# A macaron layer on one core: tile 7 of x enters its experts one position sooner, and its load moves behind the store of tile 2

## The chip, the cores and the metric

The kernel runs on one core of a Trainium2 chip. The metric is the device time of one execution in microseconds (us). The kernel before takes 1252.88 us, the median of three runs that lie between 1252.73 and 1253.44 us.

## The reference

Input x is 4 x 1024 rows of 128 numbers, all in float32. Three sublayers follow one another, each added to the row it reads:

```
x = x + 0.5 * ffn(layernorm(x))      # mixture of 8 experts
x = x + mamba(layernorm(x))          # selective scan along the 1024 rows of a sequence
x = x + 0.5 * ffn(layernorm(x))      # the same experts again

ffn(x):   cw = softmax(x @ w_router) * softmax(x @ w_gating / 0.1);  cw = cw / (sum(cw) + 1e-9)
          out = sum over e of  cw[e] * ((silu(x @ w_gate[e]) * (x @ w_up[e])) @ w_down[e])
          # w_gate, w_up: 8 x 128 x 512;  w_down: 8 x 512 x 128
mamba(x): xs, z = split(x @ W_in)                      # 256 + 256 channels
          xc = silu(conv of 4 taps along the rows(xs) + conv_b)
          dt = softplus((xc @ W_x)[:, :64] @ W_dt + b_dt);  B, C = the other 2 x 16 columns of xc @ W_x
          h[n] = exp(dt * A[n]) * h[n] + dt * xc * B[n]    # 16 states n, one row after the other
          y = sum over n of h[n] * C[n] + xc * D;   out = (y * silu(z)) @ W_out
```

Each of the two ffn sublayers uses all 8 experts for every row, so most of the arithmetic is theirs.

## The kernel before, in words

The 4096 rows are cut into 8 tiles of 512 rows (two for each sequence). An expert pass over one tile is called a position. There are 16: kind 0 is the first ffn of a tile, kind 1 the second, and the table `ORDER` (line 36) says which comes when. A tile's mamba part lies between its two passes and runs beside the positions of other tiles. It needs the tile's kind 0 output (`x1`), and its output (`x2`) is what kind 1 reads. The scan carries a state from an even tile to the odd one behind it.

A position has 32 slots, one for each of 8 experts and 4 chunks of 128 hidden columns. Chunk number i counts through all positions, so position 9 (counted from 0) has the chunks 288 to 319. In a slot TensorE (PE) does three things: the gate product of chunk i + 2 (`first_g`, lines 839 to 842, three matmuls PS<-XH,WG), the up product of chunk i (`first`, the same lines, PS<-XH,WU) and the down product of chunk i - 2 (`down`, line 920, PS<-WD,HB). Between them ScalarE (ACT) applies silu to the gate product (line 1306) and VectorE (DVE) multiplies it with the up product (line 1113, "the multiply of chunk i" from here on). The up product of chunk i + 2 goes to the PSUM bank of that of chunk i, so it waits for the multiply of chunk i. The result of each expert is weighed on ACT (line 1331) or on DVE (line 1106) and added to the tile by a transfer that accumulates (line 1439, issued by GpSimd, POOL).

The order of all instructions is not written by hand. The function `timetable()` walks through the slots with a rough clock for each engine and appends steps to one list. Every engine's program is that list, filtered, so each engine works strictly in the list's order and waits on semaphores. The steps that matter here, with their lines:

- `ln_sum`, `ln_square`, `ln_x` (1262, 1270, 1276): layernorm on ACT. `ln_sum` is the first reader of a tile, and waits for its load or for `x1` or `x2`.
- `ln_t` (861) transposes the rows on PE. `p_xh` (1284) and `p_xl` (1171) write the two halves XH from which the next position's products read.
- `b_soft` (1380, 1382): the softplus of the mamba part, with its own activation table. `b_add` (1444) and `b_dx` (1183) follow it.
- For each of the 16 states: `s_b` (1200, DVE) reads the rows of B from the ring BCB of three buffers, `s_scan` (1211, two on DVE) reads the decays DA, which `s_da` makes on ACT (1401, two states at a time), and `s_hc` (1219, DVE) multiplies with C from the same BCB buffer. The load of BCB (`bc_load`, 799) for state m is issued by SyncE (SP) once `s_hc` of state m - 3 is done. States are numbered through all tiles: tile 4 has 64 to 79.
- `out` (823) stores a finished tile, and `x_load` (816) brings in one of the tiles 5 to 7. Both are issued by SP, as are all `bc_load`s. The ring XT has five buffers, so tile 7 is loaded to the buffer of tile 2, and line 815 makes SP wait until the store of tile 2 has landed.

Of the kernel before, what the change touches and what calls it, by code (L numbers as in the profile page):

```python
# [25 lines left out]
XR = 5  # L26
# [6 lines left out]
EPS_LN = 1e-5  # L33
EPS_CW = 1e-9

ORDER = [(0, 0), (0, 1), (0, 2), (0, 3), (1, 0), (0, 4), (1, 1), (0, 5), (1, 2), (0, 6), (1, 3), (0, 7), (1, 4), (1, 5), (1, 6), (1, 7)]
NPOS = len(ORDER)
ENDS = (0, NPOS - 1)
POSITION = {kt: p for p, kt in enumerate(ORDER)}

PREP = 8
LATER = 20
LOADR = 0
LATE = 26
LEAD = 2.0
LAST = 2
# [20 lines left out]
def timetable():  # L67
# [6 lines left out]
    clock = {"pe": 0.0, "v": 0.0, "a": 0.0, "p": 0.0}  # L74
    free = [(0.0, b, None) for b in range(NB)]

    def step(*what, after=0.0, **work):

        steps.append(what)
        for e, c in work.items():  # L80
            clock[e] = max(clock[e], after) + c
            after = clock[e] + SIGNAL[e]
        return after
# [5 lines left out]
    def until(at):  # L89
        while clock["pe"] < at:  # L90
            yield False
# [5 lines left out]
    def take():  # L97
        while not free or free[0][0] > clock["pe"]:
            yield False
        return free.pop(0)[1:]  # L100
# [7 lines left out]
    def rows_of_x():  # L108

        while xn["lock"] or clock["pe"] < xn["at"]:  # L110
            yield False
        xn["lock"] = True

    def norm(b, what):
        while ln["lock"]:
            yield False
        ln["lock"] = True
        q = norms[0]
        norms[0] += 1
        yield from rows_of_x()  # L120
        yield from calm()
        if q == 0:
            at = step("ln_first", b, what, after=4.0, v=1.5, p=1.2)
            yield "first"
            at = step("ln_first_x", b, after=at, v=.7, a=.9)
        else:
            at = step("ln_sum", q, b, xn["by"], what, after=clock["pe"], a=1.6)
            yield True
            yield from calm()
            at = step("ln_square", q, b, after=at, a=1.6, p=2.0)  # L130
            yield from until(at + .3)
            at = step("ln_x", q, b, after=at, a=1.5)
        ln["lock"] = False
        yield from until(at + 0.7)
        bk = yield from take()
        at = step("ln_t", q, bk, pe=.6)
        xn.update(by=("m_tr", q + 1), lock=False)
        return q, bk[0], at

    def prep(p):  # L140
        kind, t = ORDER[p]
        q, b, at = yield from norm(t % XR, ("x", t) if kind == 0 else ("x2", t))
        at = step("p_xh", p, q, b, after=at, a=.52)
        yield from until_v(at + LATEST)
        at = step("p_xl", p, b, after=at, v=.61)
        give(b, "v_xl", p + 1, at)
        inputs.add(p)
        yield "inputs"
        yield from until(at)
        bk = yield from take()  # L150
        at = step("p_logits", p, bk, pe=.55, a=1.2)
        give(bk[0], "a_lr", p + 1, at)
        yield "logits"
        yield from until_v(at)
        at = step("p_max", p, bk[0], after=at, v=1.0)
        yield True
        if p == 0:
            yield from until(at + FIRST)
        yield from calm()
        at = step("p_exp", p, after=at, a=3.0)  # L160
        yield from until_v(at)
        at = step("p_norm", p, after=at, v=.4)
        yield True
        step("p_sum", p, v=.3)
        yield True
        at = step("p_cw", p, v=.35)
        if p in TURNS:
            streams["rows"] = weights_rows(p, at)
# [38 lines left out]
    def tail(p):  # L207
        kind, t = ORDER[p]
        if p * E + E - 1 in TURNED:
            weigh(p * E + E - 1)  # L210
        while "turn" in streams:
            yield False
        at = turned_at[p] if p * E + E - 1 in TURNED else weigh(p * E + E - 1)
        if kind == 0:
            x1[t] = at
        else:
            yield from until(at)
            step("out", t)

    def before(t):  # L220

        haste.add("before")
        q, b, at = yield from norm(t % XR, ("x1", t))
        haste.clear()
        at = step("b_xn", t, q, b, after=at, a=.52)
# [73 lines left out]
    def calm():  # L299
        while clock["a"] > clock["pe"] + CALM:  # L300
            yield False
# [59 lines left out]

    streams = {}
    rows_at, turned_at, weighed_at = {}, {}, {}
    asked = [0]

    def row_loads():
# [35 lines left out]
    def side(but=None):  # L402
        mamba_streams()
        for k in ("rows", "turn", "tail", "prep", "closing"):
            while k != but and advance(k) is True:
                pass
        decays()
        turn[0] += 1
        if "scans" in streams and (haste or turn[0] % (3 if passed[0] < NS // 2 else 1) == 0):
            advance("before")  # L410
        fill(clock["pe"] + LEAD + 1.0)

    def fill(at):

        while clock["v"] + 1.0 < at:
            mamba_streams()
            if advance("scans") is not True and advance("before") is not True:
                break
# [25 lines left out]
    def high(i):  # L444
        on = {"a": .53} if i // SLOTS in SCALAR_PARTS else {"v": .35}
        hi_at[i] = step("h_hi", i, after=h_at[i], **on)
    for i in range(total):
        p, r = divmod(i, SLOTS)
        if i + AHEAD < total:
            at = step("first_g", i + AHEAD, after=sil_at.get(i + AHEAD - NG, 0.0), pe=.69)  # L450
            sil_at[i + AHEAD] = step("silu", i + AHEAD, after=at, a=.52)
            side()
        fill(sil_at[i])
        at = step("first", i, after=h_at.get(i - 2, 0.0), pe=.69)
        clock["v"] = max(clock["v"], at, sil_at[i]) + .61
        h_at[i] = clock["v"] + SIGNAL["v"]
        if i in TURNED_SLOTS and p in SCALAR_PARTS:
            high(i)
        if i - 1 in hi_at:
            step("h_lo", i - 1, after=hi_at[i - 1], v=.6)  # L460
        if i in TURNED_SLOTS and p not in SCALAR_PARTS:
            high(i)
        side()
        if i >= LAG:
            step("down", i - LAG, after=h_at[i - LAG], pe=.7 if i - LAG in TURNED_SLOTS else .9)
            nd += 1
            if nd % FC == BEGIN_LATER and nd // FC - 1 in TURN_BEGINS:
                weigh(nd // FC - 1)
            if (nd + 1) % PAIR == 0 and nd + 1 in TURNED_SLOTS:
                on = {"a": .31} if (nd + 1) // SLOTS in SCALAR_PARTS else {"v": .2}  # L470
                step("wd_hi", nd + 1, **on)
                if "v" in on:
                    step("wd_lo", nd + 1, v=.4)
            if nd % PAIR == 0 and nd in TURNED_SLOTS and nd // SLOTS in SCALAR_PARTS:
                step("wd_lo", nd, v=.33)
            row_loads()
            if nd % SLOTS == 0:
                streams["tail"] = tail(nd // SLOTS - 1)
            elif nd % FC == 0:
                if nd % SLOTS == FC:  # L480
                    finish("prep")
                if nd // FC - 1 not in TURN_BEGINS:
                    weigh(nd // FC - 1)
        if p == 0:
            e = (r + 1) // 4 + 1
            if r % 4 == 3 and 3 <= e < E:
                step("w_split", e, (0,), a=.6, v=.7)
            e = r // 4 + 1
            if e < E and r % 4 == (0 if e < 3 else 1):
                step("w_split", e, (0, 1) if e < 3 else (1,), a=.6, v=.7)  # L490
                if e + 3 < E:
                    step("w_load", e + 3)
            if r == 6:
                step("small_load")
            if r % 2 and 25 <= r <= 29:
                step("set", (r - 25) // 2, v=1.4)
        if r == LOADR and p + 1 < NPOS and ORDER[p + 1][0] == 0 and ORDER[p + 1][1] >= XR:
            step("x_load", ORDER[p + 1][1])
        if p + 1 < NPOS and r >= (PREP if p != 1 else LATER) and p + 1 not in prepared:
            kind, t = ORDER[p + 1]  # L500
            if kind == 1 and r == LATE:
                while t not in x2:
                    side()
                    clock["pe"] += .3
            if kind == 0 or t in x2:
                prepared.add(p + 1)
                streams["prep"] = prep(p + 1)
        if r == SLOTS - 3:
            finish("prep", lambda: p + 1 in inputs)
        side()  # L510
# [973 lines left out]
```

## Time and profile before

| | us |
|---|---|
| median of three runs | 1252.88 |
| the profiled execution | 1252.7 |
| its span, first to last instruction | 1250.9 |
| PE busy / DVE busy / ACT busy / POOL busy | 1244.1 / 1131.1 / 1017.1 / 388.4 |
| PE waits that end between 130 and 1181 us of the span | 0.6 |

Times of rows are us from the start of the span. What the profiled execution's time has beyond its span, 1.8 us, lies outside the program's instructions. PE's matmuls overlap in the pipeline, and their ends are modelled, so the start of a row says more than its length: as long as PE is not held up, a slot begins every 2.28 us (the first up matmuls of two chunks stand at 751.30 and 753.58 us). The PE clock that was granted is 1.0 throughout.

### The profile page before, as it was taken

What the parts mean: (1) busy time and instruction counts of PE and PEld (TensorE: products, weight loads), DVE (VectorE), ACT (ScalarE), POOL (GpSimd) and SP (SyncE); (2) the same over time, 40 slices, a digit from 0 to 9 for tenths busy, and PEclk for the clock granted to TensorE, in tenths of its full rate; (3) what the DMA queues carried; (4) which work ended last, traced back from release to release, by engine and by line L of the source; (5) the groups of instructions that cost most, each with busy time, mean ns of one, the idle gap of its engine ahead of it and who ended that gap; (6) DMA issues with size and microseconds to landing.
All of it is one profiled execution on the core that took longest, in us unless ns stands there. A gap on an engine that the chain in (4) does not pass through costs nothing.

```text
span 1250.9 us, 20830 instructions
## 1 busy us (share of the span) xinstructions
PE 1244.1 (99%) x7311; PEld 1076.0 (86%) x7311; DVE 1131.1 (90%) x1524; ACT 1017.1 (81%) x2079; POOL 388.4 (31%) x455
## 2 busy tenths in 40 slices
PE   9999999999999999999999999999999999999998
PEld 6887888888888888888888888888888888888887
DVE  5857699999999999999999999999999989998476
ACT  6777988888987887989978899798987979765664
POOL 0010134234333333334234333352434433332100
PEclk9999999999999999999999999999999999999999
DMA  7412368797878787878898798987979887895132
GB/s 225 105 24 42 87 132 172 144 196 161 168 143 178 161 174 151 177 153 172 164 201 160 153 194 172 186 172 151 199 148 190 154 160 158 161 191 112 28 75 51
DMA packets 116809, 185.90 MB, mean 149 GB/s; under 512 B 11264, under 2 KB 31840, under 8 KB 116704
## 3 DMA queue, kind: packets, MB, share of 16 engines
q0 software_dynamic: 55760, 101.74, 46.1%
q1 hardware_dynamic: 60944, 82.83, 26.4%
q8 instruction: 57, 0.93, 0.3%
q14 instruction: 48, 0.39, 0.1%
HBM read 80.15 MB, written 2.67 MB: 66 GB/s over the span
## 4 chain that ended last, share of the span: by engine, by line
PE 96%; ACT 2%; DVE 1%; issue 1%; DMA 0%; POOL 0%; DVEq 0%; ACTq 0%
PE PS L920 32%; PE PS L839 19%; PE PS L842 19%; PE PS L840 19%; PE PS L969 1%; PE PS L954 1%; PE PS L912 1%; PE PS L914 1%; PE PS L910 1%; PE PS L861 1%; PE PS L871 1%; ACT DA L1401 0%; PE PS L961 0%; ACT HB L1306 0%; DVE HL L1069 0%
## 5 line engine op out<-in xcount | busy, mean ns | idle before, releaser
L920 PEld LDWEIGHTS PS<-WD,HB 128*128 128x128 f32 x3616 | 472.2, 191 | 37.6 <-issue 0.5
L920 PE MATMUL PS<-WD,HB 128*128 128x128 f32 x3616 | 476.0, 274 | 0.0
L1113 DVE TENSOR_TENSOR HB<-PS,HB 128x512 f32<-128x512 f32 x512 | 348.3, 681 | 85.7 <-PE PS L842 72.8
L1306 ACT ACTIVATE HB<-PS 128x512 f32<-128x512 f32 x512 | 294.6, 597 | 111.2 <-PE PS L842 108.7
L1456 POOL DMA_DIRECT2D Y<-HS x252 | 222.1, 958 | 369.2 <-DVE HS L1219 186.4
L839 PE MATMUL PS<-XH,WG 128*128 128x512 f32 x512 | 238.7, 466 | 0.8 <-DVE WG L1120 0.6
L1439 POOL DMA_DIRECT2D XT<-YE x111 | 105.4, 949 | 318.9 <-ACT YE L1331 166.8
L839 PE MATMUL PS<-XH,WU 128*128 128x512 f32 x512 | 203.7, 398 | 0.0
L842 PE MATMUL PS<-XH,WG 128*128 128x512 f32 x512 | 202.2, 395 | 0.0
L842 PE MATMUL PS<-XH,WU 128*128 128x512 f32 x512 | 201.6, 394 | 0.0
L840 PE MATMUL PS<-XH,WG 128*128 128x512 f32 x512 | 200.3, 391 | 0.0
L840 PE MATMUL PS<-XH,WU 128*128 128x512 f32 x512 | 200.3, 391 | 0.0
L1401 ACT ACTIVATE DA<-XS,aneg 128x512 f32<-128x512 f32 x256 | 164.3, 713 | 0.8
L1211 DVE TENSOR_TENSOR_SCAN HS<-DA,car,HS 128x512 f32<-128x512 f32 x128 | 161.8, 1275 | 0.0
L1219 DVE TENSOR_TENSOR HS<-BCB,HS 128x1024 f32<-128x1024 f32 x128 | 156.1, 1220 | 1.4
L1200 DVE TENSOR_TENSOR HS<-BCB,DX 128x1026 f32<-128x1026 f32 (+1 forms) x128 | 155.5, 1220 | 0.2
L1211 DVE TENSOR_TENSOR_SCAN HS<-DA,HS 128x513 f32<-128x513 f32 x128 | 153.8, 1217 | 0.1
L840 PEld LDWEIGHTS PS<-XH,WU 128*128 128x128 f32 x512 | 96.5, 188 | 22.6 <-issue 0.5
L842 PEld LDWEIGHTS PS<-XH,WU 128*128 128x128 f32 x512 | 96.0, 187 | 22.8
L839 PEld LDWEIGHTS PS<-XH,WU 128*128 128x128 f32 x512 | 96.1, 188 | 22.7 <-issue 0.5
L842 PEld LDWEIGHTS PS<-XH,WG 128*128 128x128 f32 x512 | 96.1, 188 | 22.6 <-DVE XH L1171 0.4
L1306 ACT ACT_TABLE_LOAD x87 | 111.6, 1283 | 2.1 <-PE PS L842 0.6
(133 smaller groups left out, 1343.7 us busy)
## 6 DMA issues: line engine op xcount, KB each, us to landing
BCB<-BCD SPq DMA_DIRECT2D x128, 512.0 KB, 5.3
Y<-HS POOLq DMA_DIRECT2D x252, 256.0 KB, 6.3
XT<-YE POOLq DMA_DIRECT2D x111, 256.0 KB, 4.9
YE<-CWD SPq DMA_DIRECT2D x15, 256.0 KB, 4.7
XS<-DX POOLq DMA_DIRECT2D x7, 512.0 KB, 9.0
AT<-YE POOLq DMA_DIRECT2D x11, 256.0 KB, 3.3
XT<-in_L_attn_x_dram SPq DMA_DIRECT2D x8, 256.0 KB, 6.6
WD<-in_L_ffn_w_down_dram SPq DMA_DIRECT2D x8, 256.0 KB, 6.4
```

The costliest lines, as they stand in the source:

```text
L839: pe.matmul(o, w[0], m[0], start=True, stop=False)
L840: pe.matmul(o, w[1], m[0], start=False, stop=False)
L842: pe.matmul(o, w[0], m[1], start=False, stop=True).then_inc(S[sem], 1)
L920: z = pe.matmul(part(g, j), HB[:, i % NH, j * P:(j + 1) * P], WD[:, e, c, :], start=c == 0 and j in firsts, stop=c == FC - 1 and j in lasts)
L1113: v.tensor_tensor(H, up(i), H, ALU.mult).then_inc(S["v_h"], 1)
L1200: v.tensor_tensor(HS[:, m % HR, :, 0:w], rows.unsqueeze(1).broadcast_to([P, 2, w]), DX[:, t % 2, :, 0:w], ALU.mult).then_inc(S["v_db"], 1)
L1211: v.tensor_tensor_scan(H, DA[:, m % NA, j, 0:w], H, car[:, j, n:n + 1] if t % 2 else 0.0, ALU.mult, ALU.add).then_inc(S["v_sc"], 1)
L1219: v.tensor_tensor(H, BCB[:, m % BR, 1, :].unsqueeze(1).broadcast_to([P, 2, T]), H, ALU.mult).then_inc(S["v_hc"], 1)
L1306: a.activation(HB[:, i % NH, :], gate(i), ACT.Silu).then_inc(S["a_sil"], 1)
L1401: z = a.activation(DA[:, m % NA, j, 0:T], XS[:, t % 2, j, 3:3 + T], ACT.Exp, scale=aneg[:, j, n:n + 1])
L1439: gp.dma_start(to, buffer(g), accum_op=ALU.add).then_inc(S["c_acc"], 16)
L1456: gp.dma_start(Y[:, t % 2, j, :], HS[:, m % HR, j, 0:T], accum_op=ALU.add).then_inc(S[f"c_y{j}"], 16)
```

## The change

Positions 10 and 11 change places. Before, position 10 is the second pass of tile 3 and position 11 the first pass of tile 7. Now tile 7 comes first. Its load was issued at slot 0 of the position before its pass. Now it is issued at slot 2 or later, as soon as the store of the tile five before has been issued in the list, and the clock by which `ln_sum` of the loaded tile is placed takes 7 us for that store and 8 us for the load.

```diff
-ORDER = [... (0, 6), (1, 3), (0, 7), (1, 4), (1, 5), (1, 6), (1, 7)]
+ORDER = [... (0, 6), (0, 7), (1, 3), (1, 4), (1, 5), (1, 6), (1, 7)]
...
-LOADR = 0
+LOADR = 2
+STORED = 7.0
+LOADED = 8.0
...
     def norm(b, what):
...
+        if what[0] == "x":
+            yield from until(loaded_x.get(what[1], 0.0))
         yield from rows_of_x()
         yield from calm()
...
             step("out", t)
+            stored_out[t] = clock["pe"]
...
-        if r == LOADR and p + 1 < NPOS and ORDER[p + 1][0] == 0 and ORDER[p + 1][1] >= XR:
-            step("x_load", ORDER[p + 1][1])
+        if r >= LOADR and p + 1 < NPOS and ORDER[p + 1][0] == 0:
+            t = ORDER[p + 1][1]
+            if t >= XR and t not in asked_x and t - XR in stored_out:
+                asked_x.add(t)
+                loaded_x[t] = max(clock["pe"], stored_out[t - XR] + STORED) + LOADED
+                step("x_load", t)
```

The lines of the engines' code move down by ten, so L799 becomes L809, and L1306 becomes L1316. Before position 9 only the loads of tiles 5 and 6 move, each by one or two places among the `bc_load`s. From slot 7 of position 9 on, the list differs at many places.

The first place is SP's queue around the store of tile 2, at the start of position 9. Before:

```order
L799 DMA BCB<-BCD 128x2x512 [waits v_hc] x2
L823 DMA out_dram<-XT 128x4x128 [waits c_acc]
L799 DMA BCB<-BCD 128x2x512 [waits v_hc] x4
L799 DMA BCB<-BCD 128x2x512 [waits v_hc,c_bcd]
L799 DMA BCB<-BCD 128x2x512 [waits v_hc] x3
L816 DMA XT<-in_L_attn_x_dram 128x4x128 [waits o_x]
```

Now:

```order
L809 DMA BCB<-BCD 128x2x512 [waits v_hc] x2
L833 DMA out_dram<-XT 128x4x128 [waits c_acc]
L826 DMA XT<-in_L_attn_x_dram 128x4x128 [waits o_x]
L809 DMA BCB<-BCD 128x2x512 [waits v_hc] x4
L809 DMA BCB<-BCD 128x2x512 [waits v_hc,c_bcd]
```

The load of tile 7, with its wait for the store of tile 2 (`o_x`), has moved ahead of eight BCB loads and stands right behind that store. The next BCB load behind it is that of state 76.

The second place is ACT's queue in slots 10 to 18 of position 9. Line 1262 is `ln_sum`, 1270 `ln_square`, 1380 and 1382 `b_soft` of tile 5, and 1401 makes the decays of the states 76 and 77. Before, from the silu of chunk 300 on:

```order
L1306 ACTIVATE HB<-PS 128x512
L1262 ACTIVATE XN,sums<-XT 128x128 x4
L1306 ACTIVATE HB<-PS 128x512
L1407 ACTIVATE car<-HS 128x2
L1267 ACTIVATE mean<-sums 128x4
L1270 ACTIVATE XN,squares<-XT,mean 128x128 x4
L1306 ACTIVATE HB<-PS 128x512
L1401 ACT_TABLE_LOAD
L1401 ACTIVATE DA<-XS,aneg 128x512 x4
```

Now:

```order
L1316 ACTIVATE HB<-PS 128x512
L1389 ACT_TABLE_LOAD
L1390 ACTIVATE DX<-DX 128x2x512
L1392 ACTIVATE DX<-DX 128x2x512
L1316 ACT_TABLE_LOAD
L1316 ACTIVATE HB<-PS 128x512
L1417 ACTIVATE car<-HS 128x2
L1316 ACTIVATE HB<-PS 128x512
L1272 ACTIVATE XN,sums<-XT 128x128 x4
L1316 ACTIVATE HB<-PS 128x512
L1341 ACTIVATE YE<-PS,CW 128x128 x4
L1316 ACTIVATE HB<-PS 128x512
L1417 ACTIVATE car<-HS 128x2
L1277 ACTIVATE mean<-sums 128x4
L1280 ACTIVATE XN,squares<-XT,mean 128x128 x4
L1316 ACTIVATE HB<-PS 128x512
L1411 ACT_TABLE_LOAD
L1411 ACTIVATE DA<-XS,aneg 128x512 x4
```

The softplus of tile 5 now comes ahead of the layernorm and of the decays of state 76, the weighing of expert 74 has come over from DVE, and `ln_sum` is that of the loaded tile 7, where before it was that of `x2` of tile 3.

The third place is DVE's queue from `s_b` of state 76 on. Before:

```order
L1200 TENSOR_TENSOR HS<-BCB,DX 128x2x513
L1113 TENSOR_TENSOR HB<-PS,HB 128x512
L1211 SCALAR_TENSOR_TENSOR HS<-DA,HS 128x513 x2
L1113 TENSOR_TENSOR HB<-PS,HB 128x512
L1106 TENSOR_TENSOR YE<-PS,CW 128x512
L1113 TENSOR_TENSOR HB<-PS,HB 128x512
L1219 TENSOR_TENSOR HS<-BCB,HS 128x2x512
L1200 TENSOR_TENSOR HS<-BCB,DX 128x2x513
L1113 TENSOR_TENSOR HB<-PS,HB 128x512
L1211 SCALAR_TENSOR_TENSOR HS<-DA,HS 128x513
L1113 TENSOR_TENSOR HB<-PS,HB 128x512
```

Now:

```order
L1210 TENSOR_TENSOR HS<-BCB,DX 128x2x513
L1123 TENSOR_TENSOR HB<-PS,HB 128x512
L1221 SCALAR_TENSOR_TENSOR HS<-DA,HS 128x513 x2
L1123 TENSOR_TENSOR HB<-PS,HB 128x512
L1229 TENSOR_TENSOR HS<-BCB,HS 128x2x512
L1123 TENSOR_TENSOR HB<-PS,HB 128x512
L1210 TENSOR_TENSOR HS<-BCB,DX 128x2x513
L1123 TENSOR_TENSOR HB<-PS,HB 128x512
L1221 SCALAR_TENSOR_TENSOR HS<-DA,HS 128x513
L1193 TENSOR_TENSOR DX<-XS,Y 128x2x512
L1123 TENSOR_TENSOR HB<-PS,HB 128x512 x2
```

The multiplies here are those of the chunks 300, 301, 302, 303 and 304 (and now 305). The weighing is gone from DVE, and `b_dx` of tile 5 (L1193) stands between the first scan of state 76 and the multiply of chunk 304.

## Rows read from the trace of the kernel before

**Rows 1.** The page, busy us, share of span, instructions by engine.

```profile
PE 1244.1 (99%) x7311; PEld 1076.0 (86%) x7311; DVE 1131.1 (90%) x1524; ACT 1017.1 (81%) x2079; POOL 388.4 (31%) x455
```

**Rows 2.** Waits of PE, window 130 to 1181: us, times, longest.

```profile
PE PS L961 <- ACT XS L1374: 0.4, 1, 0.4
PE PS L839 <- ACT HB L1306: 0.2, 1, 0.2
```

**Rows 3.** Positions 9 to 14: us, busy of PE, PEld, DVE, ACT, POOL, clock, DMA.

```profile
715.50:1181.40 465.90, 465.68 (x2846) 408.52 (x2845) 436.07 (x546) 378.19 (x761) 162.48 (x187) 1.00 0.80 160
```

**Rows 4.** Timeline of PE, slots 15 to 18 of position 9: start, us.

```profile
751.30 0.40 PE L839 MATMUL PS<-XH,WU 128*128 128x512 f32 x1
...
754.28 0.60 PE L861 MATMUL PS<-CON,XN 128*128 128x128 f32 x4
...
758.60 0.39 PE L839 MATMUL PS<-XH,WU 128*128 128x512 f32 x1
```

**Rows 5.** Timeline of SP around the store of tile 2.

```profile
731.62 0.47 SPq L823 DMA_DIRECT2D out_dram<-XT  x1
737.14 28.68 SPq L799 DMA_DIRECT2D BCB<-BCD  x5
```

**Rows 6.** DMA issues at 731.6: KB each, us from issue to landing.

```profile
out_dram<-XT SPq DMA_DIRECT2D x1, 256.0 KB, 8.5
```

**Rows 7.** The same at 737.1, the BCB load of state 76.

```profile
BCB<-BCD SPq DMA_DIRECT2D x1, 512.0 KB, 6.1
```

**Rows 8.** The same at 632 to 633, where tile 6 is loaded.

```profile
BCB<-BCD SPq DMA_DIRECT2D x1, 512.0 KB, 7.3
...
XT<-in_L_attn_x_dram SPq DMA_DIRECT2D x1, 256.0 KB, 10.5
```

**Rows 9.** Landing of all 128 BCB loads, line 799.

```profile
DMA to landing us min/median/max: 4.9/5.3/9.6
```

**Rows 10.** Landing of the three loads of x, line 816.

```profile
DMA to landing us min/median/max: 6.4/6.7/10.5
```

**Rows 11.** Landing of the seven `b_add` transfers, line 1444.

```profile
DMA to landing us min/median/max: 6.8/9.0/10.0
```

**Rows 12.** Timeline of DVE from `s_b` of state 76 on.

```profile
744.47 1.22 DVE L1200 TENSOR_TENSOR HS<-BCB,DX 128x1026 f32<-128x1026 f32 x1
...
748.46 0.67 DVE L1113 TENSOR_TENSOR HB<-PS,HB 128x512 f32<-128x512 f32 x1
749.04 0.68 DVE L1106 TENSOR_TENSOR YE<-PS,CW 128x512 f32<-128x512 f32 x1
...
753.47 1.22 DVE L1211 TENSOR_TENSOR_SCAN HS<-DA,HS 128x513 f32<-128x513 f32 x1
754.60 0.66 DVE L1113 TENSOR_TENSOR HB<-PS,HB 128x512 f32<-128x512 f32 x1
```

**Rows 13.** Timeline of ACT over the same slots.

```profile
739.44 1.16 ACT L1331 ACTIVATE YE<-PS,CW 128x128 f32<-128x128 f32 x4
...
740.92 0.37 ACT L1262 ACTIVATE XN<-XT 128x128 f32<-128x128 f32 x1
...
742.44 0.60 ACT L1306 ACTIVATE HB<-PS 128x512 f32<-128x512 f32 x1 [0.20 <-PE PS L842]
...
744.82 0.57 ACT L1306 ACTIVATE HB<-PS 128x512 f32<-128x512 f32 x1
745.41 1.28 ACT L1401 ACT_TABLE_LOAD   x1
746.70 2.56 ACT L1401 ACTIVATE DA<-XS,aneg 128x512 f32<-128x512 f32 x4
...
754.46 1.28 ACT L1379 ACT_TABLE_LOAD   x1
...
756.84 1.06 ACT L1382 ACTIVATE DX<-DX 128x1024 f32<-128x1024 f32 x1
```

**Rows 14.** Timeline of POOL, the last Y transfer of state 74.

```profile
746.30 0.86 POOL L1456 DMA_DIRECT2D Y<-HS  x1 [0.38 <-DMA Y<-HS]
```

More of the change, by code:

```diff
@@ L34 @@
 EPS_CW = 1e-9
-ORDER = [(0, 0), (0, 1), (0, 2), (0, 3), (1, 0), (0, 4), (1, 1), (0, 5), (1, 2), (0, 6), (1, 3), (0, 7), (1, 4), (1, 5), (1, 6), (1, 7)]
+ORDER = [(0, 0), (0, 1), (0, 2), (0, 3), (1, 0), (0, 4), (1, 1), (0, 5), (1, 2), (0, 6), (0, 7), (1, 3), (1, 4), (1, 5), (1, 6), (1, 7)]
 NPOS = len(ORDER)
@@ L363, in timetable @@
     rows_at, turned_at, weighed_at = {}, {}, {}
+    asked_x, stored_out, loaded_x = set(), {}, {}
     asked = [0]
```

## The prediction

> **What bounds the kernel now.** I read the busy shares first. PE is busy for 1244.1 of the 1250.9 us of the span, DVE for 90% of it and ACT for 81% [rows 1]. Then I asked who PE waits for, between the end of the opening and the last position. The reader is to see that there is next to nothing: 0.4 and 0.2 us in a thousand [rows 2]. The table of stretches says the same of the positions 9 to 14, where the change acts. There PE is busy 465.68 of 465.90 us, and DVE 436.07, which is 94% [rows 3]. Last I read the timelines of PE, SP, DVE and ACT in the slots 10 to 18 of position 9, since that is where the order first differs in more than a place or two, and the lengths of the DMAs there.
>
> Two things follow. PE sets the time. The change adds and removes no product, so the time can fall only by waits that go, and these are at most 0.6 us [rows 2]. And DVE has 6% to spare in this stretch, so a delay on DVE reaches PE as soon as it is longer than the lead that the multiplies have over the up products.
>
> That lead can be read. The up product of chunk 303 starts at 751.30 us [rows 4] and needs the multiply of chunk 301, which ends at 748.46 + 0.67 = 749.13 [rows 12]: 2.2 us. The up product of chunk 306 starts at 758.60 and needs the multiply of chunk 304, over at 755.26: 3.3 us. There the four transposes of the second tile's rows, 0.60 us long and overlapped, precede it at 754.28 [rows 4]. In the new order they come later, so chunk 306 starts some 0.4 us sooner, at 758.2, if PE is not held up.
>
> **Part 1: the load of tile 7 on SP.** Before, the store of tile 2 is issued at 731.62, and SP's next issue, the BCB load of state 76, goes out at 737.14, when DVE has freed the buffer [rows 5]. The store lands 8.5 us after its issue, at 740.1 [rows 6], and nobody in SP's queue cares. Now the load of tile 7 stands between the two and waits for that landing. It is issued at 740.2 and takes SP 0.47 us, as the store did [rows 5]. So the BCB load goes out at 740.7, 3.5 us later than before. Behind it on SP stand only the loads of later states, whose buffers are freed later anyway (that of state 77 at about 744).
>
> The BCB load took 6.1 us there [rows 7], and 7.3 us where a load of x ran beside it [rows 8]. A load of x now runs ahead of it, so I take the middle, 6.7, and it lands at 747.4. Bounds are 4.9 and 9.6 us [rows 9], which give 745.6 and 750.3. DVE wants it at 744.47 [rows 12]. So `s_b` of state 76 starts 2.9 us late (1.1 to 5.8), and so do the multiplies in line behind it, 300 first. For chunk 301 the lead is 2.2 us. PE stops for about 0.8 us, counting 0.1 for the signal (0 to 3.7).
>
> The Trainium skill says in DMA: Bandwidth & Descriptors, section "Anatomy of one DMA — SWDGE (gpsimd) path", that a DMA's fixed cost is about 2.0 us, mostly the write receipt, and that a semaphore is waited for on the issuing sequencer. The second half is the mechanism of this part. By the first, a store of 256 KB would be down long before 737.14 and this part would cost nothing. The row says 8.5 us, in a stretch where the DMA engines are 80% busy [rows 3], and I go by the row.
>
> **Part 2: ACT's order.** The softplus of tile 5 has moved ahead of the decays. I add up the new queue from the end of the silu of chunk 300, 740.92 [rows 13]. Table load, Exp and Ln take 756.84 + 1.06 - 754.46 = 3.4 us, the table back 1.3, two silus and a `car` copy 1.3: 746.9. There ACT meets `ln_sum` of tile 7. The tile lands at 740.2 + 6.7 = 746.9 [rows 10], just in time. `ln_sum` 1.3 (740.92 to 742.24), silu 0.6, the weighing of expert 74 1.2, silu 0.6, `ln_square` with its copies 1.8 (744.82 - 742.44 - 0.6), silu 0.6, table 1.3, and half of the four decays 1.3: the decays of state 76 stand at 755.6. DVE comes there at 747.4 + 9.0 (744.47 to 753.47) - 0.7 for the weighing that has left its queue [rows 12] = 755.7. So ACT and DVE meet, and the scan waits for nothing more. Without part 1 it would wait for ACT instead: the two delays lie beside each other and don't add.
>
> Behind the first scan comes `b_dx`. It wants the `b_add` transfer. POOL can issue that behind the last Y transfer, at about 747.2 [rows 14], and 9.0 us make 756.2 [rows 11]; DVE is there at 755.7 + 1.1 = 756.8. At the 10.0 of rows 11 it would be 0.4 late. `b_dx` itself takes 1.2 us, like the other elementwise operation of its width in rows 12. So the multiply of chunk 304 runs from 758.0 to 758.7, and the up product of chunk 306 is due at 758.2 + 0.8 = 759.0. No further stop, but a lead of only 0.3 us.
>
> ScalarE: Activation LUTs of the Trainium skill, section "What ACT_TABLE_LOAD costs", gives 2.66 us for a switch of table set, 1.38 of it a drain behind the load. Three switches lie on the new ACT queue up to the decays, so by that they would come 4.1 us later and PE would stop for some 4 us more. The trace disagrees: the load of 1.28 us at 745.41 is followed by its first decay at 746.70 [rows 13].
>
> **Part 3: the rest of the reordering.** The positions 10 to 14 hold the same instructions in another mixture. In the old mixture PE waited 0.6 us in all from 130 us on [rows 2], with the same 94% on DVE. I put the new one at the same value, within 0.6 less and 1.5 more. The moves of the loads of tiles 5 and 6 meet stores that landed long ago and cost SP 0.5 us each, as before. PE has the same products to run and sits in front of no queue but its own, so its share of the reordering I cost at nothing.
>
> **The sum.** 0.8 + 0 + 0 = 0.8 us more waiting on PE. The profiled execution took 1252.7 us, so its like is 1253.5. The median of the runs lies 0.2 above that execution: 1253.7 us.
>
> **The rivals.**
>
> A: the new waits are long. The wait of SP for the store, and behind it the load of tile 7, are one chain, and ACT stands at its end. If tile 7 takes the 10.5 us of tile 6 [rows 8], it lands at 750.7, ACT waits 3.8 us in `ln_sum`, the decays come at 759.4, and the multiply of chunk 304 ends at 762.4 instead of by 758.2: PE stops 4 us in all, 1252.9 + 4 = 1256.9. If the BCB load takes 9.6 us it is 3.7 us [rows 9]. It becomes slower than I can tell from no change once tile 7 lands more than 9.2 us after its issue, or the BCB load more than 8.4. For it: one of three loads did, a BCB load is right behind this one, and the 512 KB of `b_add` now fall into the same 10 us. Against it: two of three took 6.4 to 6.7.
>
> B: no cost. The store lands sooner than 8.5 us, or DVE catches up, as its lead of 2.2 us nearly covers 2.9. Then the time is 1252.9, and 1252.3 if the old waits go too. The Trainium skill's fixed cost of a DMA (part 1) would bring this case about.
>
> C: the new mixture of positions 10 to 13 makes waits of its own. DVE is 94% busy there, and a place where three long DVE operations stand between two multiplies costs what exceeds a lead of about 2.2 us. Two or three such places, at 0.8 each like part 1, with part 1 itself: 1255 to 1255.5.
>
> D: it gets faster by more than 0.2%. No wait of that size exists before the last position [rows 2], and the tail behind it is the same code.
>
> **Chances.** Forecast 0.50, A 0.20, B 0.17, C 0.10, D 0.03. A measurement of this kernel can tell 0.2%, 2.5 us, from no change, so the bounds are 1250.4 and 1255.4. Slower holds A and about half of C: 0.25. Faster is D: 0.03. Within 0.2% is what is left, 0.72. The range from 1252.3 (B) to 1256.6 takes in most of A and leaves out D and A's far end. The forecast's own range is 1253.0 to 1254.9.
>
> **What would show it.** Right: in the new trace the load of tile 7 is issued at the moment the store of tile 2 lands, the BCB load of state 76 goes out 0.5 us later, near 740.7, `s_b` of state 76 has idle time before it that ends with a DMA, and PE's waits in position 9 come to about 1 us. `ln_sum` of tile 7 has little or no wait. Wrong: a BCB load that lands before 746, so that PE never stops (B), an ACT that stands 2 us or more before `ln_sum` (A), or PE waits that lie in the positions 10 to 13 (C).

## The result and the profile after

| | before | after |
|---|---|---|
| median of 8 runs each, us | 1252.91 | 1256.68 |
| lowest to highest | 1252.20 to 1253.44 | 1255.94 to 1256.91 |
| profiled execution, its span | 1252.7, 1250.9 | 1256.9, 1255.1 |

The ratio is 1.0029, with a 95% interval from 1.0020 to 1.0039: the kernel became slower, by 3.8 us between the medians. I had forecast 1253.7, and had given "slower by over 0.2%" a chance of only 0.25. The measured median lies 0.1 us above the upper end of my range (1256.6), and the ratio stands at that end (1256.6 over 1252.88 is 1.0030). One run of experiment 5 below took 2541.7 us, for a reason that no record shows, and counts in no number here.

PE's busy time is the same but for what pipelined matmuls show when they wait, and the other engines do the same work. This is the page of after, the line that answers to [rows 1]:

```profile
PE 1245.9 (99%) x7311; PEld 1076.3 (86%) x7311; DVE 1131.5 (90%) x1526; ACT 1015.7 (81%) x2071; POOL 387.5 (31%) x455
```

The positions 9 to 14 of after, with the columns of [rows 3]. The window starts and ends at the same place in PE's order, so its length compares with the 465.90 there:

```profile
715.99:1185.12 469.13, 466.35 (x2846) 408.45 (x2845) 436.55 (x548) 376.74 (x753) 161.00 (x187) 1.00 0.78 159
```

It is 3.2 us longer, at the same granted clock, with DVE's and POOL's busy time within 1.5 us and ACT's 1.5 us less. The two profiled executions differ by 4.2 us. Of the other 1.0, one half lies before the window and one half behind it; executions of one list differ by as much, and the loss in the window is waiting, not work. The waits of PE in after, for the window of [rows 2]:

```profile
PE PS L871 <- ACT XN L1286: 1.2, 1, 1.2
PE PS L849 <- DVE HB L1123: 1.1, 1, 1.1
PE PS L849 <- ACT HB L1316: 0.4, 1, 0.4
PE PS L971 <- ACT XS L1384: 0.4, 1, 0.4
```

Two stops of over 1 us are new, and each is one event. PE's timeline has them: the four transposes of tile 7 in position 9, and the up product of chunk 414 in position 12.

```profile
758.79 0.50 PE L849 MATMUL PS<-XH,WU 128*128 128x512 f32 x1
...
760.99 0.63 PE L871 MATMUL PS<-CON,XN 128*128 128x128 f32 x4 [1.24 <-ACT XN L1286]
...
1027.87 0.51 PE L849 MATMUL PS<-XH,WU 128*128 128x512 f32 x1 [1.13 <-DVE HB L1123]
```

The first row is the up product of chunk 306, which stood at 758.60 in [rows 4]. It comes 0.16 us late (2.44 us behind that of chunk 305, where 2.28 is the spacing). The whole execution is 0.5 us later than that of before by then.

**The first stop.** What the prediction computed did happen. SP's timeline in after, beside [rows 5]:

```profile
732.11 0.47 SPq L833 DMA_DIRECT2D out_dram<-XT  x1
740.38 0.37 SPq L826 DMA_DIRECT2D XT<-in_L_attn_x_dram  x1
740.80 4.03 SPq L809 DMA_DIRECT2D BCB<-BCD  x2
```

The load of tile 7 waits for the landing of the store, 8.3 us after its issue (8.5 in [rows 6]), and the BCB load of state 76 goes out at 740.80 (forecast 740.7). Then both transfers are quicker than I took them to be. These are the DMA issues of after between 740.0 and 741.2, KB and us to landing:

```profile
BCB<-BCD SPq DMA_DIRECT2D x1, 512.0 KB, 5.1
XT<-in_L_attn_x_dram SPq DMA_DIRECT2D x1, 256.0 KB, 2.9
```

DVE in after, beside [rows 12]:

```profile
745.91 1.23 DVE L1210 TENSOR_TENSOR HS<-BCB,DX 128x1026 f32<-128x1026 f32 x1 [0.87 <-DMA BCB<-BCD]
...
749.91 0.66 DVE L1123 TENSOR_TENSOR HB<-PS,HB 128x512 f32<-128x512 f32 x1
...
755.79 1.23 DVE L1221 TENSOR_TENSOR_SCAN HS<-DA,HS 128x513 f32<-128x513 f32 x1 [1.75 <-ACT DA L1411]
756.94 1.20 DVE L1193 TENSOR_TENSOR DX<-XS,Y 128x1024 f32<-128x1024 f32 x1
758.05 1.28 DVE L1123 TENSOR_TENSOR HB<-PS,HB 128x512 f32<-128x512 f32 x2
```

`s_b` of state 76 starts 1.4 us later than in [rows 12], not 2.9. The multiply of chunk 301 ends at 750.57, and the up product that needs it, of chunk 303, is at 751.79, so PE is not held. The scan then waits 1.75 us for ACT, and the multiply of chunk 304 starts at 758.05 (forecast 758.0). ACT's timeline shows why it is late, and what comes of it:

```profile
753.06 1.28 ACT L1411 ACT_TABLE_LOAD   x1
754.36 2.57 ACT L1411 ACTIVATE DA<-XS,aneg 128x512 f32<-128x512 f32 x4
756.94 1.28 ACT L1316 ACT_TABLE_LOAD   x1
758.24 1.09 ACT L1316 ACTIVATE HB<-PS 128x512 f32<-128x512 f32 x2
759.21 1.64 ACT L1286 ACTIVATE XN<-XT,nm,rs 128x128 f32<-128x128 f32 x4
```

Behind the decays stand a table load, two silus and `ln_x` of tile 7, which ends at 760.85. The transposes want it, and they stand on PE right behind the up product of chunk 306, whose last matmul starts at 759.36. The decays were at 746.70 in [rows 13]. They are 7.7 us later, and so are the silus behind them and `ln_x` (751.55 in before, 759.21 now).

**The second stop.** The chain of waits before chunk 414, in order of time: start, us, what.

```profile
1006.55 1.22 DVE HS L1229
...
1008.05 6.57 DMA Y<-HS
...
1015.15 0.86 POOL Y L1466
...
1016.78 9.12 DMA XS<-DX
...
1025.99 0.06 DVE DX L1193
...
1027.13 0.70 DVE HB L1123
...
1027.87 0.51 PE PS L849
```

A Y transfer takes 6.6 us. Behind it on POOL stands `b_add` of tile 7, which takes 9.1 us, and `b_dx` of tile 7 on DVE waits 2.6 us for it, ahead of a multiply that PE wants. The planner reckons 7.0 us for `b_add`. All seven of before took 6.8 to 10.0 [rows 11].

To say where the small losses are, I add up over all pairs of neighbouring matmuls in a position how much longer the second starts after the first than the median of the same pair in before. In us, by position:

| | 9 | 10 | 11 | 12 | 13 | 14 | sum |
|---|---|---|---|---|---|---|---|
| before | -0.07 | -0.12 | 0.21 | 0.29 | 0.22 | -0.11 | 0.4 |
| after | 1.62 | 0.09 | 0.59 | 1.47 | 0.02 | 0.09 | 3.9 |

The difference of 3.5 is more than the 3.2 of the window, since the exchange also changes which matmuls are neighbours, and a rare pair has few others to be compared with. So the sums are good to some tenths: with pairs told apart by line, operands and shapes, position 12 of before comes to -0.25, and no other entry moves by more than 0.2. The difference lies in the positions 9 (1.7), 12 (1.2, or 1.7 by the other count), 11 (0.2 to 0.4) and 10 (0.2). I call this sum "the excess" below.

### The profile page after: what moved, and what is told of

Same layout as the page of the kernel before. It is cut to its first block, busy times and chain, and to the rows that moved or that the text cites. A ratio compares the mean times of both kernels' runs of the same rounds, so it can differ in the third digit from the quotient of the medians.

```text
span 1255.1 us, 20828 instructions
## 1 busy us (share of the span) xinstructions
PE 1245.9 (99%) x7311; PEld 1076.3 (86%) x7311; DVE 1131.5 (90%) x1526; ACT 1015.7 (81%) x2071; POOL 387.5 (31%) x455
## 4 chain that ended last, share of the span: by engine, by line
PE 89%; ACT 4%; DVE 3%; DMA 2%; issue 2%; POOL 0%; DVEq 0%; ACTq 0%; POOLq 0%
PE PS L930 29%; PE PS L849 18%; PE PS L852 17%; PE PS L850 17%; DMA Y<-HS 2%; PE PS L979 1%; PE PS L922 1%; PE PS L924 1%; PE PS L964 1%; PE PS L920 1%; PE PS L871 1%; ACT HB L1316 1%; DMA XS<-DX 1%; ACT DA L1411 1%; DVE HB L1123 1%
## 5 line engine op out<-in xcount | busy, mean ns | idle before, releaser
L1316 ACT ACTIVATE HB<-PS 128x512 f32<-128x512 f32 x512 | 294.8, 597 | 115.0 <-PE PS L852 112.4
```

Source lines behind the costliest of these rows:

```text
L1316: a.activation(HB[:, i % NH, :], gate(i), ACT.Silu).then_inc(S["a_sil"], 1)
```

## The experiments

Each was timed in five rounds beside runs of before on the same chip. The chips differ between experiments, but the medians of before on them lie between 1252.75 and 1252.93, so medians of different experiments can be set side by side to some 0.2 us.

**1. The load rule alone**, with the old order of positions.

```diff
-LOADR = 0
+LOADR = 2
+STORED = 7.0
+LOADED = 8.0
 (and the rest of the diff, without ORDER)
```

> The old table of positions with the new rule for the loads of x. Theory (the cost comes from the new mixture of steps in the positions 9 and 12, not from the rule): like the kernel before, 1252.9 within 0.5 us, PE's waits behind 130 us as before. Rival (a load of x tied closely to a store costs by itself, wherever it stands): 1 us or more above before.

Measured: 1252.94 against 1252.93, ratio 0.9999 (0.9991 to 1.0008). The excess is that of before. The new rule costs nothing by itself. All of the loss belongs to the exchange of positions and to the list that the planner makes of it.

**2. The load of tile 7 behind the BCB load of state 76**, all else as in after.

```diff
+    behind(("x_load", 7), ("bc_load", 76))   # in the finished list
```

> The changed kernel, but the load of tile 7 stands behind the BCB load of state 76 in SP's queue, not ahead of it. Theory (the stop of 1.4 us in position 9 is PE's transposes waiting for ln_x, which ACT reaches late): SP's wait is gone, s_b of state 76 starts 0.9 us sooner without idle time, the decays of state 76 and ln_x stand where they were, and the time stays within 0.4 us of the changed kernel's 1256.7. Rival (the wait of SP for the store is what makes all behind it late, my part 1): 1 to 1.5 us less, 1255.3.

Measured: 1256.36, ratio 1.0028 (1.0018 to 1.0037). The BCB load is issued at 737.4 again, and 0.3 us come back, which cannot be told from nothing. The excess of position 9 is as in after (1.7). So part 1 of the prediction, the mechanism that I had built the forecast on, is not what costs.

**3. The load of tile 7 early, in the kernel before.** This is part 1 by itself.

```diff
+    place(("x_load", 7), ("out", 2))   # before, finished list
```

> The kernel before, with one step moved: the load of tile 7 stands right behind the store of tile 2 in SP's queue, two positions before it is needed. Only SP's wait for the store is new. Rival (my part 1: the BCB load of state 76 goes out 3.5 us late and lands after DVE wants it, and PE stops 0.8 us): 1253.7. Theory (a BCB load behind this wait lands in 5.1 us as in the changed kernel, DVE starts 1 to 1.5 us late, which the lead of 2.2 us covers): 1252.9, at most 0.3 more.

Measured: 1253.07 against 1252.83, ratio 1.0000 (0.9991 to 1.0009). Its SP and DVE timelines:

```profile
740.23 0.37 SPq L824 DMA_DIRECT2D XT<-in_L_attn_x_dram  x1
740.65 4.14 SPq L807 DMA_DIRECT2D BCB<-BCD  x2
```

```profile
745.76 1.23 DVE L1208 TENSOR_TENSOR HS<-BCB,DX 128x1026 f32<-128x1026 f32 x1 [0.75 <-DMA BCB<-BCD]
```

The same delay on SP and the same idle time on DVE as in after, and PE does not notice: its excess in position 9 is 0.08. With this and experiment 2, the stop of 0.8 us of the prediction is shown not to exist, in the old list and in the new one.

**4. The transposes one slot later.**

```diff
+    behind(("ln_t", 16), ("first", 307))   # after, finished list
```

> The changed kernel, but PE's four transposes of tile 7's rows stand one slot later, behind the up product of chunk 307. Theory: the wait for ln_x (1.2 us on the row of the transposes) goes and 1.2 to 1.4 us of time with it, 1255.4. Rival (PE would be stopped by a multiply there anyway, since DVE is as late as ACT): the wait turns up at the up product of chunk 308 or 309 and the time stays at 1256.7.

Measured: 1256.79, ratio 1.0029 (1.0018 to 1.0041). The theory's 1255.4 is missed. The wait at the transposes is gone, and the excess of position 9 falls from 1.62 to 0.96. Half a us of this 0.96 is new: two products around chunk 312 start late, as they do in 6 and 7, where the transposes are moved too. The positions 10 (by 0.4) and 12 (from 1.47 to 1.83) take back the rest of what 9 gave, and the sum is 4.0. This is PE's timeline in position 12:

```profile
1027.23 0.51 PE L857 MATMUL PS<-XH,WU 128*128 128x512 f32 x1 [1.49 <-DVE HB L1131]
```

PE waits there for the multiply behind `b_dx` of tile 7, and that waits for `b_add`, which took 9.5 us here and 9.1 in after. Counted from the start of position 9, PE comes 0.3 us sooner than in after and waits 0.4 longer.

**5. `b_add` of tile 7 reckoned at 9.5 us in the planner.** It moves `b_dx` of tile 7 some places back on DVE.

```diff
-            at = step("b_add", t, after=at, p=.9) + 7.0
+            at = step("b_add", t, after=at, p=.9) + (9.5 if t == 7 else 7.0)
```

> The changed kernel, but the transfer b_add of tile 7 is reckoned with 9.5 us in the order's clock, not 7, so that b_dx of tile 7 stands one scan and two multiplies later in DVE's queue. Theory (the stop of 1.3 us in position 12 is DVE waiting 2.6 us in b_dx for that transfer, with the multiplies behind it): 1.1 to 1.3 us less, 1255.5, and no wait of DVE on XS<-DX there. Rival (DVE has no lead left in position 12 and PE is stopped by the amount of work on DVE): the wait of PE moves to a later slot and the time stays.

Measured: 1254.90, ratio 1.0014 (1.0005 to 1.0023), 1.8 us less than after, where 1.1 to 1.3 were expected. The excess of position 12 falls from 1.47 to 0.06, and the positions 13 and 14 have 0.4 less between them. DVE's `b_dx` of tile 7 has no idle time before it:

```profile
1025.36 1.22 DVE L1193 TENSOR_TENSOR DX<-XS,Y 128x1024 f32<-128x1024 f32 x1
```

`b_add` of tile 7 took only 8.0 us in this profile, so a part of this may be the transfer's. But it took 8.7 and 8.8 us in 6 and 7, which have the same edit, and position 12 has no stop there either.

**6. The edits of 2, 4 and 5 together.**

> The changed kernel with all three edits: the load of tile 7 behind the BCB load of state 76, the transposes a slot later, b_add of tile 7 reckoned with 9.5 us. Theory (in position 9 DVE is nearly as late as ACT, so the transposes' wait only hides a wait for a multiply; the two edits there are worth 0.3 us each and b_dx's is worth 1.8): 1254.3. Rival (the edit of the transposes was worth its 1.4 us all along, and the stop in position 12 took it back, being tied to a transfer and not to PE): 1253.2.

Measured: 1254.81 against 1252.83, ratio 1.0015 (1.0007 to 1.0024). Both expectations missed: there is no gain over 5. The two edits of position 9 take a wait away from the transposes, but DVE waits 2.3 us for the decays all the same, and the excess of position 9 is still 1.37, of which 0.5 us stands at the up product of chunk 306 and as much around chunk 312. To move the step that waits is no cure.

**7. The same, with the decays of state 76 right behind the silu of chunk 302.**

```diff
+    place(("s_da", 76), ("silu", 302))   # 6, finished list
```

> As e5, and the decays of the states 76 and 77 stand right behind the silu of chunk 302 on ACT, ahead of the layernorm of tile 7. Theory (what is left in position 9 comes from DVE waiting 1.8 us for the decays of state 76, behind softplus and layernorm): that wait of DVE is gone, and 0.8 to 1.2 us of time with it against e5, near 1253.2. Rival (ACT as a whole is too full there, so what the decays gain the layernorm loses): PE waits at the transposes again and the time is that of e5 or more.

Measured: 1255.54, ratio 1.0021 (1.0012 to 1.0030), slower than 6. ACT has too much to do in these slots: the decays are sooner and a silu is late. This is PE's timeline:

```profile
753.79 0.50 PE L859 MATMUL PS<-XH,WG 128*128 128x512 f32 x1 [0.98 <-ACT HB L1326]
```

**8. The kernel before with every `b_add` reckoned at 9.0.**

```diff
-            at = step("b_add", t, after=at, p=.9) + 7.0
+            at = step("b_add", t, after=at, p=.9) + 9.0
```

> The kernel before, with b_add of every tile reckoned with 9.0 us (the middle of its seven landings) and not 7: does the mended clock make a better order of the old table too? Theory (PE waits 0.6 us in all behind 130 us, of which little is from b_dx): 1252.9 within 0.5. Rival (any reshuffle of the order makes a stop or two of about 1 us): 1 to 2 us more.

Measured: 1282.34, ratio 1.0234 (1.0220 to 1.0248), 29.5 us slower, against both expectations. One wait at the end of position 14 is most of it. This is from the waits of PE, and below it is the stretch right behind that wait, with the columns of [rows 3]:

```profile
PE PS L969 <- DVE Y L1233: 20.4, 3, 19.2
```

```profile
1186.49:1192.30 5.81, 5.81 (x22) 5.33 (x23) 0.69 (x1) 1.28 (x9) 0.00 (x0) 0.50 0.00 0
```

The wait costs more than its length. The granted clock falls to 0.50 (the level of 1.2 GHz) while PE stands still, PE runs the next 5.8 us at that clock, and after a second stop, of 2.8 us, another 3.4 us. By half of these, an estimate, the clock costs 4.6 us.

A more truthful duration for a transfer gave a much worse list, since the scan of the last tile now ends late. So the constants of this planner cannot be judged one by one by how true they are.

**9. The softplus of tile 5 held back in the planner**, with the `b_add` of 5. ACT then does the decays of state 76 and `ln_sum` and `ln_square` of tile 7 first. Not `ln_x`: it still stands behind the softplus. And the planner puts the transposes that want it two slots later, behind the up product of chunk 308. So the hold moves both the step ahead and one that waits.

```diff
+        if t == 5:
+            yield from until(755.0)
         yield from calm()
         at = step("b_soft", t, after=at, a=4.5)
```

> The new order with b_add of tile 7 reckoned at 9.5 us (as in e4), and the softplus of tile 5 held back in the planner until its clock reads 755, so that ACT does the decays of state 76 and the layernorm of tile 7 first, as it did before the change. Theory: the stop of 1.4 us at the transposes of tile 7 in position 9 comes from the 4.7 us (two table loads, Exp, Ln) that the softplus puts ahead of decays, ln_square and ln_x on ACT. With it behind them ln_x ends some 4 us sooner, the transposes wait for nothing, position 9 falls from 1.6 us over the old spacing to 0.3 or less, and the time falls by 1.3 to 1.6 from 1254.9 to about 1253.4. Rival: DVE is the cause (s_b of state 76 is 1.5 us late behind its load), so the stop stays whatever ACT's order is: no change, 1254.9. Second rival: the softplus only moves the stop to the gate product behind it, as the decays did in e6: 1254.8 to 1255.5.

Measured: 1254.01 against 1252.89, ratio 1.0008 (0.9999 to 1.0017), which can no longer be told from before. It is 0.9 us less than 5, where 1.3 to 1.6 were expected. ACT's timeline:

```profile
742.54 1.28 ACT L1413 ACT_TABLE_LOAD   x1
743.84 2.57 ACT L1413 ACTIVATE DA<-XS,aneg 128x512 f32<-128x512 f32 x4
...
755.71 1.06 ACT L1392 ACTIVATE DX<-DX 128x1024 f32<-128x1024 f32 x1
...
759.76 1.64 ACT L1288 ACTIVATE XN<-XT,nm,rs 128x128 f32<-128x128 f32 x4
```

PE's transposes:

```profile
762.88 0.60 PE L873 MATMUL PS<-CON,XN 128*128 128x128 f32 x4
```

and the waits of PE from 130 to 1200 us:

```profile
PE PS L973 <- ACT XS L1386: 0.5, 2, 0.4
PE PS L851 <- DVE HB L1125: 0.3, 1, 0.3
```

The scan of state 76 waits for nothing, although `s_b` of state 76 still waits for its load (1.26 us). The excess is 0.48 in position 9 and 0.6 in all. But the profiled execution took 1253.03 us, near the fastest of the eleven (1253.01 to 1255.25) and 1.0 under their median, so it shows the better case of this list; 11 shows another. With 2 and 3, this makes ACT's order the cause in position 9, and not the load. How much of it the earlier decays give and how much the later transposes, 9 doesn't separate; the transposes moved alone (4, 6) left 0.96 and 1.37 there.

**10. A load of x reckoned at 2.5 us instead of 8.0**, with the `b_add` of 5. The softplus falls behind the layernorm by the planner's own rules.

```diff
-LOADED = 8.0
+LOADED = 2.5
```

> The new order with b_add of tile 7 reckoned at 9.5 us, and a load of x reckoned at 2.5 us behind its store's landing instead of 8.0 (it took 2.9 in the new kernel). The planner then puts the layernorm of tile 7 ahead of the softplus again: ln_sum, ln_square, the decays of state 76, ln_x, and the softplus of tile 5 behind them. Theory: as for e9, but ln_sum is queued on ACT near 742, 1 to 1.5 us before the tile is there (743.3 in the new kernel); the silus behind it have a lead of about 1 us before the multiplies want them, so PE loses 0 to 0.8 us there and gains the 1.4 at the transposes: 1253.4 to 1254.2. Rival: ln_sum's wait reaches PE in full and the time stays at 1254.9 or goes up to 1255.5 (as when the load is slow, 6 us and more: then 3 us or more are lost).

Measured: 1257.05, ratio 1.0031 (1.0019 to 1.0043), outside what either expected. Position 9 went as in the theory. ACT waits 1.8 us in `ln_sum` for the tile, PE 0.45 us at the transposes, and the excess is 0.77:

```profile
743.38 0.31 ACT L1272 ACTIVATE XN<-XT 128x128 f32<-128x128 f32 x1 [1.80 <-DMA XT<-in_L_attn_x_dram]
```

But the list differs from there on, and positions 11 and 12 hold five stops of 0.4 to 0.8 us (the one in position 11 stands in before too), 3.6 us in position 12's excess. One of DVE's waits behind them is again that for `b_add` of tile 7, which took 10.5 us where 9.5 were reckoned:

```profile
979.83 1.23 DVE L1210 TENSOR_TENSOR HS<-BCB,DX 128x1026 f32<-128x1026 f32 x1 [1.11 <-DMA BCB<-BCD]
988.62 1.23 DVE L1221 TENSOR_TENSOR_SCAN HS<-DA,HS 128x513 f32<-128x513 f32 x1 [1.27 <-ACT DA L1411]
...
1014.70 1.23 DVE L1193 TENSOR_TENSOR DX<-XS,Y 128x1024 f32<-128x1024 f32 x1 [2.58 <-DMA XS<-DX]
```

**11. The softplus held back, `b_add` reckoned at 7.0.** Against after, only the hold is new. PE's order is that of 9 up to position 12.

> The new order with the softplus of tile 5 held back as in e9, but b_add of tile 7 reckoned at 7.0 us as in the new kernel: it differs from e9 in position 12 alone, where b_dx of tile 7 stands one multiply sooner in DVE's queue. Theory: the two stops are separate and add up. The one of position 9 is gone as in e9, the one of position 12 (1.3 us at a gate product, behind b_dx of tile 7 that waits for b_add) is back: PE in position 12 is 1.2 to 1.7 us over the old spacing again, and the time is 1254.0 + 1.6 = 1255.6. Rival: the stop of position 12 has a fixed end, the landing of b_add, so what is gained in position 9 is waited for there, as in e3: the whole of it comes back and the time is 1256.3 to 1256.8.

Measured: 1254.15 against 1252.75, ratio 1.0012 (1.0003 to 1.0021). Holding one step back takes 2.5 us of the 3.8 away, more than either expectation had. In its profile the stop of position 12 is not there (excess -0.32): `b_dx` of tile 7 waits 0.57 us only,

```profile
1015.23 1.57 POOL L1456 DMA_DIRECT2D XS<-DX  x1
...
1022.58 1.23 DVE L1195 TENSOR_TENSOR DX<-XS,Y 128x1024 f32<-128x1024 f32 x1 [0.57 <-DMA XS<-DX]
```

since `b_add` landed after 7.3 us, where it took 8.9 to 9.5 in after, 2 and 4. And position 9 has a stop of another kind, 1.6 us at chunk 312, where `b_dx` of tile 5 waits 2.9 us for its `b_add` (1.7 in 9, whose profile shows 0.3 us on PE for it):

```profile
774.12 0.51 PE L851 MATMUL PS<-XH,WU 128*128 128x512 f32 x1 [1.56 <-DVE HB L1125]
```

This is the price of the hold: `b_add` of tile 5 comes behind the softplus and is issued at 762.68, where it was 749.30 in after. The excess of position 9 is about 1.8, as much as in after, and it is all that this execution (1254.61 us) lost. So the hold removed the stop at the transposes in both profiles, but the cost of position 9 in one of them only. Whether the transfer of tile 7 is short in every execution of this list, or in this one, I can't tell from one profile.

No version beat before. Its own waits from 130 us on are 0.6 us [rows 2], so there was nothing to win that a measurement could show.

## Why the prediction was wrong in its steps

The measured time stands at the edge of my range, but that is luck. The range reached so far only for rival A, whose mechanism was not there. In the terms of the sum, 0.8 + 0 + 0 came out as 0 for part 1, 1.7 in position 9 (part 2) and 1.8 in the positions 10 to 14 (part 3).

**The bound and the sign: right.** PE sets the time, there is no room for a gain, and a delay on DVE or ACT reaches PE once it is longer than the lead. Both new stops are of this kind.

**Part 1, 0.8 us: mis-sized, it is 0.** The times on SP were right within 0.2 us. The BCB load took 5.1 us instead of my 6.7, so `s_b` was 1.4 us late instead of 2.9, and the lead of 2.2 us for chunk 301 covered it. Experiments 2 and 3 show it from both sides. I took the middle of two rows, 6.1 and 7.3. The median of all 128 such loads stood in [rows 9], 5.3. The Trainium skill's fixed cost of a DMA (DMA: Bandwidth & Descriptors, section "Anatomy of one DMA — SWDGE (gpsimd) path") would have given the right 0 here for the wrong reason: the store landed 8.3 us after its issue, not 2. (That section is on transfers issued by GpSimd, and SP issued this one.)

**Part 2, "no further stop": the step that failed.** The queue of ACT was added up to the decays with the right end (755.6; the scan started at 755.79), though it began 0.6 us later than I took it and its terms came to 0.6 less. DVE's own sum was 1.7 too late (it stood ready at 754.04, since the BCB load was quick), and the multiply of chunk 304 came as forecast (758.0 against 758.05) only because ACT's sum gave the same time. That I had written: without part 1 the scan would wait for ACT. I stopped there. The same sum goes on: end of the decays 756.9, table 1.3, two silus 1.1 with overlap, `ln_x` 1.6, so 760.9, and the transposes of tile 7, which I had noted "come later", are due at 759.6. That is 1.2 us on PE and could be worked out from the new list and the trace of before. Below it lies the cause: the softplus, 4.7 us on ACT with its two table loads, stands ahead of the decays and the layernorm. Experiments 9, 10 and 11 move it back, and the stop of the scan for the decays goes in each. The edits that treat only what it delays gain nothing: 4 nothing over after, 6 nothing over 5, and 7 loses.

**Part 3, 0 with a margin of 1.5: wrong.** The new mixture of positions 10 to 14 costs 1.8 us of excess, outside that margin. Of this 1.2 is the stop in position 12, where `b_dx` of tile 7 waits for a `b_add` that the planner reckons too short. Experiment 5 took it away and got 1.8 us back. Before reckons the same 7.0, and its `b_add` took longer too [rows 11]: there `b_dx` of tile 7 waits 0.7 us for it, and the lead of the multiplies behind covers that. The remaining 0.6 of positions 10 and 11 I have not traced further than to a silu that is 0.4 us late.

**The rivals.** A has nearly the time (1256.9) by a mechanism that was not there: tile 7 came in 2.9 us, and ACT never waited for it. B was right about part 1. C had the place, waits in the positions 10 to 13, though I gave it 0.10 and 1255 to 1255.5, and its mechanism, three long operations on DVE in a row, is not what the stop of position 12 is: DVE waits there for a transfer. The time is made of a stop in position 9 that I had worked out by half, and of this one.

**The signs.** All that I had named as signs of being right appeared: the load at the landing of the store, the BCB load near 740.7, `s_b` idle until a DMA, no wait of `ln_sum`, and about 1 us of PE's waits in position 9. The last did so by luck, since these 1.2 us stand at the transposes and not at a multiply. Two signs of being wrong appeared as well: the BCB load landed before 746 (740.80 + 5.1 = 745.9), and PE waited in position 12. A sign that gives only an amount and a position doesn't tell one mechanism from another.

**What stays open.** The hold alone returns 2.5 us (11), the `b_add` alone 1.8 (5), both 2.7 (9), so they overlap, and I have shown the overlap only in one profile, by a transfer that landed sooner. The 1.1 us by which 9 lies above before can't be told from nothing.

## What to carry to other kernels

When a change reorders in-order queues, add up each queue past the first meeting point, until the engine that sets the time has taken its next operand of every kind. Here the end of the sum was right to 0.2 us, in part because two errors of 0.6 us cancelled, and the sum ended one step too early. A list made with reckoned durations hides transfers that take longer than reckoned behind whatever lead happens to be there, and each new list draws these leads anew. So "the same work in another mixture" has a cost on a kernel whose second engine is 94% busy: here 0 to 2.5 us between lists that differ by one constant or one held step, 3.7 for the exchange of two positions, and 29 us in one case. Where a stop is found, look for the step that is ahead of its releaser in the queue and could be elsewhere: moving the waiting step or the releaser moved the stop. Moving the step ahead removed it, and then that step's own readers (`b_add` and `b_dx` of tile 5) have to be added up too.

## What the runs showed of the hardware that I had not expected

- The load of tile 7, 256 KB from HBM, issued just behind the landed store, took 2.9 us in after and 2.8 to 4.0 in the nine experiments that issue it there (2 to 7 and 9 to 11), where the three of before took 6.4 to 10.5 [rows 10]. The BCB load issued 0.4 us behind it in after landed after 5.1. Why it is so quick here is not shown.
- The store of 256 KB ahead of it took 7.9 to 8.6 us in after and in these experiments (8.5 before), while the median of the seven stores in after is 5.4:

```profile
DMA to landing us min/median/max: 4.9/5.4/8.3
```

- The accumulating 512 KB `b_add` of tile 7 took 7.3 to 10.7 us in the different lists (7.3 in 11, 10.7 in 8). It stood on the chain of the stop in position 12, and that of tile 5 (8.9 us) on the chain of the stop in 11.
- ACT switches tables without a gap also under this load: in after the load of 1.28 us at 753.06 is followed by the first decay at 754.36. By ScalarE: Activation LUTs of the Trainium skill, section "What ACT_TABLE_LOAD costs", it would start 1.4 us later. The trace decides.
- A stop of 19.2 us on PE was followed by work at a granted clock of 0.50 (experiment 8), while the stops of up to 1.6 us in after, 4 and 11 left the clock at 1.00.
